# A graph kernel's VectorE addition stops waiting for POOL's gather five tiles ahead

## The reference

```
deg = max(number of edges into each node, 1)
S[n, r, :]  = sum of x[src] over the edges with dst = n and type = r
cnt[n, r]   = number of those edges
agg[n]      = sum over r of S[n, r, :] @ relation_weights[r]  +  cnt[n] @ rFeatures
h           = agg * deg ** -0.5
h           = relu(h + h @ loop_weight)
out         = layernorm(x + h)
```

## Time and profile before

| what | value |
|---|---|
| median of 3 runs | 1065.96 us |
| profiled execution, its own time | 1067.09 us |
| its span, first to last instruction | 1065.2 us |
| TensorE busy, mean granted clock | 963.2 us (90%), 0.986 |
| TensorE weight loads | 856.5 us (80%) |
| POOL busy | 788.1 us (74%) |
| VectorE busy | 735.1 us (69%) |
| ScalarE busy | 529.9 us (50%) |
| DMA | 127.27 MB, mean 119 GB/s |

### The profile page before, as it was taken

How to read it: one execution, slowest core, us unless ns; L and a number is a source line. 1 busy time by engine, 2 the same in 40 slices (tenths; PEclk the granted TensorE clock), 3 DMA queues, 4 the chain that set the end, 5 groups by cost and what they waited for, 6 DMA issues and landing times.

```text
span 1065.2 us, 26678 instructions
## 1 busy us (share of the span) xinstructions
PE 963.2 (90%) x6713; PEld 856.5 (80%) x6713; DVE 735.1 (69%) x2572; ACT 529.9 (50%) x1119; POOL 788.1 (74%) x832
## 2 busy tenths in 40 slices
PE   3589999998999999999999999999999999989997
PEld 1379988888888788888888888888887888878887
DVE  7687777666766766676667666666766676767663
ACT  3566554454545445544444544455454554444552
POOL 7777777777777777777777777777777777777770
PEclk9779999999999999999999999999999999999999
DMA  8933344434433444444344444444433344333430
GB/s 271 303 89 107 113 114 115 115 113 117 117 115 113 116 115 114 113 117 116 112 117 114 117 113 115 116 115 112 114 112 110 111 114 114 110 112 110 114 112 25
DMA packets 68987, 127.27 MB, mean 119 GB/s; under 512 B 17287, under 2 KB 41582, under 8 KB 68830
## 3 DMA queue, kind: packets, MB, share of 16 engines
q0 software_dynamic: 38400, 103.80, 34.5%
q1 hardware_dynamic: 16398, 15.38, 4.6%
q10 hardware_dynamic: 14032, 6.35, 2.1%
HBM read 115.85 MB, written 9.60 MB: 118 GB/s over the span
## 4 chain that ended last, share of the span: by engine, by line
PE 50%; DMA 25%; POOL 15%; issue 7%; DVE 1%; POOLq 0%; SPq 0%; ACT 0%; DVEq 0%; ACTq 0%
PE win_ps L1103 25%; DMA rows<-x_parts,src 24%; PE agg_ps L1115 21%; POOL rows L557 13%; POOL raw L564 2%; PE win_ps L1141 1%; DMA x_in<-x 1%; PE win_ps L1188 1%; PE win_ps L1089 1%; PE win_ps L1140 0%; POOLq L556 0%; DVE hot L856 0%; SPq L461 0%; DVE ring L989 0%; DMA src<-src_main 0%
## 5 line engine op out<-in xcount | busy, mean ns | idle before, releaser
L557 POOL DMA_INDIRECT rows<-x_parts,src x766 | 732.5, 956 | 234.4 <-issue 156.2
L653 ACT COPY ring<-win_ps 128x451 f32 x831 | 465.7, 560 | 383.1 <-PE win_ps L1103 187.9
L1103 PE MATMUL win_ps<-hot,rows 128*128 128x480 f32 x1634 | 566.1, 431 | 60.9 <-DMA rows<-x_parts,src 53.7
L1115 PEld LDWEIGHTS agg_ps<-ring,w 128*128 128x128 f32 x3936 | 554.2, 191 | 41.9
L1115 PE MATMUL agg_ps<-ring,w 128*128 128x128 f32 x3936 | 562.2, 275 | 0.0
L989 DVE TENSOR_TENSOR ring<-ring,win_ps 128x41 f32 x831 | 188.6, 227 | 307.9 <-DMA rows<-x_parts,src 220.0
L856 DVE TENSOR_SCALAR hot<-iota,key_f 128x480 fp32r<-128x480 f16 x831 | 384.0, 462 | 1.0 <-issue 1.0
L1103 PEld LDWEIGHTS win_ps<-hot,rows 128*128 128x128 f32 x1634 | 251.1, 193 | 98.4 <-DMA rows<-x_parts,src 86.5
L1089 PEld LDWEIGHTS win_ps<-hot_node,hot_type 128*128 128x128 bf16 x831 | 77.1, 100 | 42.0 <-issue 15.7
L1089 PE MATMUL win_ps<-hot_node,hot_type 128*128 128x12 bf16 x831 | 86.0, 171 | 19.9 <-DVE ring L989 12.1
L564 POOL DMA_INDIRECT raw<-x,src x51 | 53.7, 1054 | 15.6 <-issue 14.0
(11 more groups left out here) (93 smaller groups left out, 251.6 us busy)
## 6 DMA issues: line engine op xcount, KB each, us to landing
x_out<-x_parts SPq DMA_DIRECT2D x1674, 1.0 KB
rows<-x_parts,src POOLq DMA_INDIRECT x766
x_parts<-x_out SPq DMA_DIRECT2D x6, 512.0 KB, 6.5
x_parts<-ring SPq DMA_DIRECT2D x6, 512.0 KB, 6.5
out<-out_sb ACTq DMA_DIRECT2D x48, 64.0 KB
x_blk<-x ACTq DMA_DIRECT2D x47, 64.0 KB
w<-relation_w SPq DMA_DIRECT2D x8, 320.0 KB
x_in<-x SPq DMA_DIRECT2D x6, 256.0 KB
```

Source lines behind the costliest of these rows:

```text
L557: pool.indirect_dma_start(rows[0:n, k].rearrange("p c d -> p (c d)").bitcast(F32), None, x_parts, bass.IndirectOffsetOnAxis(ap=src[0:n, t: ...
L653: nc.scalar.copy(ring[:, :, bass.ds(start + 1, WIN - 1)], win_ps[bank_of(t)][:, :, 1:WIN]).then_inc(copied, 1)
L1103: ins = nc.tensor.matmul(banks[bank_of(t)][:, 0:R * WIN], of[:, part], hot[:, t % HOTS], start=False, stop=(part == PARTS - 1), skip_group ...
L1115: ins = nc.tensor.matmul(sums_of(c), w[:, r, :], ring[:, r, bass.ds(seg, BLOCK)], start=(r == 0), stop=(r == COLS - 1))
```

## The change

From tile 48 on, the wait for the gather is not issued. The addition then follows ScalarE's copy (and whatever stands ahead of it in VectorE's own order). For tiles 0 to 47 the wait stays as it was; `min(..., USED - 1)` is dropped since it never binds there.

```diff
 LEAD, LEAD_STEP = 17, 4
+PACED = 48
...
                         a = ring[:, :, bass.ds(start, 1)]
-                        last = min(t + max(BEHIND, LEAD - t // LEAD_STEP), USED - 1)
-                        dve.wait_ge(gather_issued, gathers_through(last))
+                        if t < PACED:
+                            last = t + max(BEHIND, LEAD - t // LEAD_STEP)
+                            dve.wait_ge(gather_issued, gathers_through(last))
                         nc.vector.tensor_tensor(a, a, win_ps[bank_of(t)][:, :, 0:1], ALU.add).then_inc(added, 1)
```

## The result

The changed kernel takes 1083.79 us (median of 4 runs, 1082.6 to 1086.9) against 1065.43 us for the kernel before in the same runs (median of 4). The ratio is 1.018, 95% interval 1.0168 to 1.0192. It is slower by 18 us. The forecast was slower by 35, with a range of 1078 to 1112 us.

A forecast was written before the change was run, and what follows sets the result against it. The prediction took POOL's back-to-back gathers as the bound. The profiled execution's 1067.09 us plus 35 us of longer gathers made 1102, and as that execution was 1.1 us above the median, the forecast was 1101 us, range 1078 to 1112.

The forecast's parts named there:

- The bound: POOL's gathers run back to back, one every 1.257 us; only gather length and the 26.6 us tail can move the time.
- The wait's idle time is worth nothing: VectorE's 220.0 us of waiting at line 989 buys nothing when removed, since neither TensorE nor POOL waits for VectorE there.
- The one-hot and the gather exclude each other at two places: VectorE's one-hot against POOL's gather: whoever comes second waits, at two places in a gather, at most some 0.24 us.
- the first place: Just before a gather's start: a one-hot 0.13 us ahead went with a gather of 1.14 us.
- the second place: Inside a running gather: a one-hot 0.60 us after its start went with a gather of 1.19 us.
- the rival "faster": Earlier additions remove long gathers whose one-hot fell about 0.4 us in: 2 to 5 us gained, 1061 to 1064; chance 0.05.
- The price, 0.0483 us for each one-hot: Excess gather time of 2.32 us over 48 one-hots in the free stretch, carried to 728 in the held stretch: 35.2 us.
- The forecast's own band, 25 to 46 us: Loss from longer gathers once one-hots are free, giving 1091 to 1112 us; chance 0.63.
- the partial lock: Copies repeat every 17 tiles, so one-hots may favour harmless places in gathers: 10 to 24 us lost, 1076 to 1090; chance 0.17.
- The check from the shape, 33 us: Sensitive widths of 0.27 and 0.20 us in a 1.257 us pitch, mean delay 0.12 us, over 728 one-hots: 33 us.
- The rival that a one-hot keeps the gather out to its reported end: A one-hot in progress delays the gather until it ends: 61 us for one place, time 1113 to 1128; chance 0.07.
- rival D: Named with the experiments: pacing VectorE by a wait helps wherever the wait is put; no chance given.

The follow-up runs named there:

- light_one_port_free: light_free with the one-hot reading its positions from 15 rows of 32 with gaps, inferred to use one SBUF port (0.70 us instead of 0.46): 1291.38 us.
- light_free: The changed kernel with three relations per matmul and one load for each row-loaded tile, leaving out part of the computation: 1292.72 us.

## Why the prediction was right, and where its size was off

**The bound.** Right. POOL ran back to back before and after (0.305 us between gathers both times), and the end moved by 16.9 us for 17.7 us of longer gathers, less 0.8 us of idle time between them. Where POOL paused, the lengths of its gathers did not show in the time: light_one_port_free has 28 us less of gathers than light_free and took 1291.38 us against 1292.72, which can't be told apart (its VectorE also does 190 us more).

**The wait's idle time is worth nothing.** Right: line 989's 220.0 us of waiting went over to the copy, and ScalarE's 52.3 us went without a gain.

**The one-hot and the gather exclude each other at two places.** Right, and shown by the one-port form: 84 to 109 gathers a run with a one-hot at the first place, at 0.945 or 0.946 us on the mean. But the row for the second place was misread. The gather of 1.19 us at 105.90 had another one-hot, begun 0.11 us before its start:

```profile
105.79 0.47 DVE L856 TENSOR_SCALAR hot<-iota,key_f 128x480 fp32r<-128x480 f16 x1
```

So its delay belongs to the first place, and a one-hot 0.60 us in costs a gather nothing. There is a second place, but at 0.38 to 0.48 us, where the rival "faster" had seen it (about 0.4 us). That VectorE's other operations take part is right too; those with two SBUF sources made 5.4 of the 22.7 us. The price of at most some 0.24 us does not hold for them: up to 0.56 us.

**The price, 0.0483 us for each one-hot.** This is the term that was mis-sized. It measured (0.9778 - 0.9521) x 715 = 18.4 us over 727 one-hots, 0.0253 each. The 39 gathers between 87.5 and 138.8 us were no fair sample. VectorE was catching up there, and its one-hots came in close pairs: 13 of 39 gathers had a one-hot at the start place, one in three, and six of the 13 a second one 0.36 to 0.62 us in. In the steady part after the change it is 109 of 716, one in 6.6. The price of a hit was about the same, 2.06 us on those 13 (0.16 each) and 15.2 us on the 109 (0.14 each). So it was the frequency and not the price. The forecast's own band, 25 to 46 us, was missed; the stated range held because it also took in the partial lock.

**The check from the shape, 33 us.** It agreed with the 35 us by luck. I took the second place as 0.20 us wide with a mean delay of 0.12, from the misread row. The curve after has a delay only from 0.38 to 0.48 us, at most 0.11; beyond it POOL comes first and the one-hot pays. With 0.23 us at 0.12 and 0.10 at 0.05 the same formula gives 728 x (0.23 x 0.12 + 0.10 x 0.05) / 1.257 = 19 us. It counts one-hots alone, which made 17.0 us of the excess after and 2.8 us before; that it comes near 18.4 is luck as well, since the operations with two sources are in that.

**The rivals.** The time fell into the band of the partial lock (1076 to 1090, given 0.17). Part of its reason holds: in the steady part the share of delayed gathers varies with the tile's place in its step of 17, from 2% at place 4 to 60% at place 16 (counted from 0; delayed is over 0.96 us). But the one-hots lie all over the pitch; it is no lock. The rival that a one-hot keeps the gather out to its reported end is refuted: 1.15 us at -0.12, not 1.28.

**What stays open.** That the loss of 18 us goes away with the one-port one-hot was not seen in a time, for want of a chip without stalls; it rests on the lengths of the gathers. The cause of the stalls is open. So is a one-hot locked at a bad place, and with it rival D: no run held its one-hots at another place. So are the operations with two SBUF sources, which no kernel changed. The late one-hots that the kernel before has once in each step (the 52 gathers of the third class, 2.8 us in all) would be the next thing to take away; it wasn't tried.

## What to carry to other kernels

A wait that looks idle can be doing work: here it kept VectorE's one-hots of 0.46 us out of the two places of a gather at which they lengthen it. Look at the lengths of the bounding engine's own instructions, not only at its waits, before taking such a wait away; a maximum far above the median, as 1187 ns over 950, is the sign. A price taken from a short stretch must be split into how often and how much, since the first seldom carries over.

## What was not expected of the hardware

The exclusion goes both ways within one gather. The turn from the gather waiting to the one-hot waiting lies about 0.1 us before the gather's recorded start, and again about 0.5 us in: a one-hot begun 0.12 us ahead made the gather 1.15 us long, while one begun 0.52 us in took 0.66 us itself and left the gather at 0.945. A gather that waits at its start waits until shortly before the recorded end of the other: the one-hot begun 0.12 us ahead ends at 0.34, and the gather took 0.2 us more; the merge that began with the gather ends at 0.66, and it took 0.53 us more.

The same kernel took 1065 us in one set of runs and 1345 to 1371 us in others, with pauses of some 2 us about once in 10. With 1530 matmul instructions for the sums in place of 3936, and one load for each row-loaded tile, it took 1296 us, and the pauses stayed.

The Trainium skill ("SBUF — State Buffer", "Who interferes with whom") says that `tensor_scalar` can enter a mode that takes both ports, when its operands meet that mode's conditions, and that it then excludes GpSimd. The pair of one-hots with and without the gap in the source agrees: 0.46 against 0.70 us, and 1.15 against 0.945 us for the gather. By the same section whoever issues first has the ports for its whole instruction. On VectorE's side the waits above come near that; on POOL's they do not: a one-hot begun 0 to 0.24 us into a gather ran inside it at its usual 0.46 us.
